# Attention over 8 images: filler products before the first projection, and exact weights for VectorE's low parts kept in an idle bank of sums

## The chip, the core and the metric

One NeuronCore of a Trainium2 chip runs the whole program. The time is the device time of one execution in microseconds; it is compared by medians over several executions of each kernel.

## The reference, cut to what matters

For each of 8 images with 128 channels and 32 x 32 = 1024 pixels, the program computes self-attention over the pixels:

```python
q = einsum('oc,bcn->bon', Wq, xf) + bq      # 64 x 1024 per image
k = einsum('oc,bcn->bon', Wk, xf) + bk      # 64 x 1024
v = einsum('oc,bcn->bon', Wv, xf) + bv      # 128 x 1024
attn = softmax(einsum('bci,bcj->bij', q, k), axis=-1)   # 1024 x 1024
out  = gamma * einsum('bcn,bmn->bcm', v, attn) + x
```

All inputs and the output are fp32.

## The kernel before, in words

TensorE works with rounded fp32r and bf16 operands, so each factor is split into a high part and a low part (the rest). An exponential is therefore made twice by ScalarE: `weight` (exact, fp32) and `weight_hi` (rounded to fp32r). Their difference, `weight_lo` (bf16), is made by GpSimd (POOL) in three steps of four and by VectorE (DVE) in the fourth.

**The work.** There are 128 steps, 16 for each image. A step `s` has 2 tiles of keys by 256 queries, 512 columns of scores in all. Four steps make a part `u` (`PART_STEPS` = 4): a part has 256 queries, and its sums fill two of the four PSUM banks called `sums`: banks 0 and 1 for even `u`, 2 and 3 for odd `u` (`part_banks`). The PSUM has 8 banks: two of `scores`, four of `sums`, two of `work`.

**One step.** TensorE makes the scores (`score_tile`, L592 and L593: four products of 256 columns). ScalarE makes the exact weights (L776) and the rounded ones (L779). POOL (L469) or DVE (L878) subtracts. TensorE adds the high parts to the sums two steps later (`sums_hi`, L612: four products of 258 columns), and once per part all four low parts (`sums_lo`, L626: sixteen products of 130 columns). DVE has the low part of step 2 of each part from part 1 on (`low_on_dve`, 31 steps); POOL has the other 97.

**Beside it.** Softmax needs the largest score of each row first. TensorE makes the high scores of a later chunk into a bank of `work` (L548, 120 products of 512 columns) and DVE takes the maximum (L840). Further jobs on the two banks of `work` are the projections of the next images: q and k (L535 to L537) and v (L542). A bank is handed on when DVE has read it, so TensorE waits for DVE there. The steps 0 to 17 have more maxima than the later ones, up to two each (`EARLY_MAXES`), because the maxima run ahead by nearly two chunks.

**Order.** Each engine has its own list, written out by the step loop `for s in range(ALL_STEPS)`. In loop `s` TensorE does the scores of step `s + 2`, the maxima of `max_jobs(s)`, `sums_hi(s - 2)`, and, where `s - 2` ends a part, `sums_lo`; then side jobs. ScalarE does both exponentials of step `s + 2`. DVE does side jobs, the maxima of loop `s`, then `low_weights(s + 1)` where that step is its own, then `invert` and `add_low` of a part that has just ended (L889, L883), then `finish` (L903), which writes the output tile and counts `y_done`. `sums_hi` of the first step of part `u` waits until part `u - 2`, the last user of its banks, has been finished (`y_done`).

**The start.** POOL sets `identity` (a memset L420, then a select L422); TensorE waits for it and turns it `WARM_UP` = 10 times into bank 0 of `sums` (`keep_busy`, L632), a transpose of 128 columns each. Then come the first three projections k0, q0, k1 (L641: fp32 products of 512 columns, each two instructions, when the loads of x and of the weights have landed), whose results ScalarE takes up (L790, L794). VectorE has nothing to do until k0 has been taken up.

Of the kernel before, what the change touches and what calls it, by code (L numbers as in the profile page):

```python
# [11 lines left out]
HALVES = PIXELS // CHUNK  # L12
# [8 lines left out]
PAIR = 2  # L21
PART = PAIR * TILE
PARTS = CHUNKS * CHUNK_TILES // PAIR
PART_STEPS = ALL_STEPS // PARTS
# [7 lines left out]
IDENTITY_MADE = 2  # L32
SETUP_MADE = 14

WARM_UP = 10

FIRST = ["k0", "q0", "k1", "q1"]

# [1 line left out]
DVE_LOW = 2  # L40
# [55 lines left out]
def low_on_dve(s):  # L96
    return s >= PART_STEPS and s % PART_STEPS == DVE_LOW


def low_count(s):  # L100

    return sum(low_on_dve(i) == low_on_dve(s) for i in range(s + 1))
# [27 lines left out]
def half_count(n, h):  # L130

    return HALVES * (n - 1) + h + 1
# [6 lines left out]
def wait(engine, semaphore, count):  # L139
    if count > 0:  # L140
        engine.wait_ge(semaphore, count)


def attention_program(nc, x, x_turned, w_turned, biases, bv, gamma, out):
    fp32 = mybir.dt.float32
    fp32r = mybir.dt.float32r
    bf16 = mybir.dt.bfloat16
    ALU = mybir.AluOpType
    ACT = mybir.ActivationFunctionType
# [4 lines left out]
    with ExitStack() as ctx:  # L154
        def sbuf(name, shape, dtype):
            return ctx.enter_context(nc.sbuf_tensor(name, shape, dtype))

        def psum(name, shape, dtype):
            return ctx.enter_context(nc.psum_tensor(name, shape, dtype))

        def sem(name):
            return ctx.enter_context(nc.semaphore(name))

        identity = sbuf("identity", [128, 128], fp32)
        identity_r = sbuf("identity_r", [128, 128], fp32r)
        w_v_plain = sbuf("w_v_plain", [CHANNELS, CHANNELS], fp32)
        w_qk_t = sbuf("w_qk_t", [CHANNELS, 2 * HEAD], fp32)
# [29 lines left out]
        weight = sbuf("weight", [TILE, RING, CHUNK], fp32)  # L197
        weight_hi = sbuf("weight_hi", [TILE, RING, CHUNK], fp32r)
        weight_lo = sbuf("weight_lo", [TILE, RING, CHUNK], bf16)
# [6 lines left out]
        scores = psum("scores", [TILE, 2, CHUNK], fp32)  # L206
        sums = psum("sums", [TILE, CHUNK_TILES, CHUNK], fp32)
# [16 lines left out]
        pool_setup = sem("pool_setup")  # L224
# [27 lines left out]
        max_rows_done = sem("max_rows_done")  # L252
        max_row_sent = [sem(f"max_row_sent{p}") for p in range(2)]

        first_lo_done = sem("first_lo_done")
        qk_lo_done = sem("qk_lo_done")
        v_lo_done = sem("v_lo_done")
# [2 lines left out]
        weight_lo_done = sem("weight_lo_done")  # L260
# [4 lines left out]
        y_done = sem("y_done")  # L265
# [13 lines left out]
        def part_tile(kt, it):  # L279

            return slice(kt * PART + it * TILE, kt * PART + (it + 1) * TILE)

        def part_banks(u):
            return slice(u % 2 * PAIR, (u % 2 + 1) * PAIR)

        def key_tile(s, kt):
            return s % PART_STEPS * PAIR + kt
# [30 lines left out]
        def wait_low(engine, s):  # L318
            engine.wait_ge(weight_lo_done if low_on_dve(s) else weight_lo_pool_done, low_count(s))

        def wait_lo_summed(engine, s):

            if s >= 0:
                engine.wait_ge(sums_done, s // PART_STEPS + 1)
# [182 lines left out]
        def _(pe):  # L507
# [88 lines left out]
            def sums_hi(s):  # L596
                b, k = divmod(s, STEPS)
                u, j, p, r = s // PART_STEPS, s % PART_STEPS, b % 2, s % RING
                if k in (0, 2):
                    if b > 0:  # L600
                        pe.wait_ge(v_lo_done, half_count(b, k // 2))
                    elif k == 0:
                        pe.wait_ge(first_v_lo_done, 1)
                    else:
                        pe.wait_ge(first_v_rest_done, 1)
                if j == 0:

                    wait(pe, y_done, PAIR * (u - 1))
                pe.wait_ge(weight_hi_done, s + 1)
                for kt in range(PAIR):  # L610
                    for it in range(PAIR):
                        last = pe.matmul(sums[:, u % 2 * PAIR + it, 0:VCOLS], weight_hi[:, r, part_tile(kt, it)],  # L612
                                         values[p][:, key_tile(s, kt)], start=(j == 0 and kt == 0), stop=False)
                last.then_inc(hi_step, 1)
# [14 lines left out]

            def keep_busy(turns, place):  # L630
                for _ in range(turns):
                    pe.transpose(place[:, 0:128], identity[:, :], identity[:, :])  # L632

            pe.wait_ge(pool_setup, IDENTITY_MADE)
            keep_busy(WARM_UP, sums[:, 0])

            def project_first(name):
# [47 lines left out]
            for s in range(ALL_STEPS + LAG):  # L685
                if s + AHEAD < ALL_STEPS:
                    score_tile(s + AHEAD)
                if s < ALL_STEPS:
                    for c, i in max_jobs(s):
                        do_max(c, i)  # L690
                if s < PART_STEPS:
                    if s == 0:

                        pe.wait_ge(neg_max_done, CHUNK_TILES + PAIR)
                    sums_hi(s)
                elif PART_STEPS + LAG <= s < ALL_STEPS:
                    if s == PART_STEPS + LAG:

                        pe.wait_ge(qk_lo_done, HALVES)
                    sums_hi(s - LAG)  # L700
                if LAG <= s < ALL_STEPS and (s - LAG) % PART_STEPS == PART_STEPS - 1:
                    sums_lo(s - LAG)
                if s == 1:
                    pe.wait_ge(neg_max_done, MAXES)
                    project_qk(1, 0, sums[:, PAIR + 1])
                if s == 2:
                    pe.wait_ge(first_v_rest_done, 1)
                    project_qk(1, 1, sums[:, PAIR])
                if s < ALL_STEPS:
                    for job in side_jobs(s):  # L710
                        do_job(job)


            p, u = (BATCHES - 1) % 2, PARTS - 1
            pe.wait_ge(weight_hi_done, ALL_STEPS)
            for it in range(PAIR):
                place = sums[:, u % 2 * PAIR + it]
# [13 lines left out]
        def _(act):  # L731
# [39 lines left out]
            def exponentials(s):  # L771
                r = s % RING
                act.wait_ge(scores_done, s + 1)
                if s >= RING:
                    wait_low(act, s - RING)
                act.activation(weight[:, r], scores[:, s % 2], ACT.Exp)  # L776

                wait(act, hi_step, s - RING + 1)
                act.activation(weight_hi[:, r], scores[:, s % 2], ACT.Exp).then_inc(weight_hi_done, 1)  # L779

            def take_low_sum(u):
                act.wait_ge(sums_done, u + 1)

                wait(act, total_done, u - 1)
                act.activation(low_sum[:, u % 2], sums[:, part_banks(u), 0:CHANNELS], ACT.Copy).then_inc(low_sum_done, 1)  # L785
# [19 lines left out]
            act.wait_ge(pool_setup, SETUP_MADE)  # L805
            write_max_rows(1, 0, 0, PART, bank(0))
            exponentials(0)
            first_q(1, bank(0))
            round_v(0, 1, sums[:, PAIR])
            exponentials(1)  # L810

            for s in range(ALL_STEPS):
                b, k = divmod(s, STEPS)
                if s + AHEAD < ALL_STEPS:
                    exponentials(s + AHEAD)
                if s in (1, 2):
                    round_qk(1, s - 1, sums[:, PAIR + 2 - s])
                if s >= LAG and (s - LAG) % PART_STEPS == PART_STEPS - 1:
                    take_low_sum((s - LAG) // PART_STEPS)
                for job in side_jobs(s):  # L820
                    do_job(job)
                if k in X_HI_STEPS and b + 2 < BATCHES:
                    round_x(b + 2, X_HI_STEPS.index(k))
# [4 lines left out]
        def _(dve):  # L828
# [45 lines left out]
            def low_weights(s):  # L874
                r = s % RING
                dve.wait_ge(weight_hi_done, s + 1)
                wait_lo_summed(dve, s - RING)
                dve.tensor_tensor(weight_lo[:, r], weight[:, r], weight_hi[:, r], ALU.subtract).then_inc(weight_lo_done, 1)  # L878

            def add_low(u):  # L880
                dve.wait_ge(low_sum_done, u + 1)
                place = sums[:, part_banks(u), CHANNELS:2 * CHANNELS]
                dve.tensor_tensor(place, place, low_sum[:, u % 2], ALU.add).then_inc(total_done, 1)  # L883

            def invert(u):
                dve.wait_ge(low_sum_done, u + 1)

                wait(dve, y_done, PAIR * (u - 1))
                dve.reciprocal(one_over[:, u % 2], sums[:, part_banks(u), 2 * CHANNELS]).then_inc(one_over_done, 1)  # L889

            def finish(u):
# [9 lines left out]
                for it in range(PAIR):  # L901
# [2 lines left out]
                                             one_over[:, u % 2, it:it + 1], x_turned_sb[:, n % TURNED, h * CHUNK_TILES + at],  # L904
                                             ALU.mult, ALU.add).then_inc(y_done, 1)

            dve.wait_ge(biases_loaded, 16)

            def first_lo(h):
# [32 lines left out]
            for s in range(ALL_STEPS):  # L942
# [10 lines left out]
                if s >= LAG and (s - LAG) % PART_STEPS == PART_STEPS - 1:  # L953
                    u = (s - LAG) // PART_STEPS
# [6 lines left out]
            u, half = PARTS - 1, 1  # L961
# [54 lines left out]
```

## Time and profile before

| | |
|---|---|
| median of 3 executions | 231.02 us (230.31 to 231.49) |
| the profiled execution, its own time | 231.92 us |
| its span, first to last instruction | 230.1 us |
| TensorE (PE) busy | 223.4 us, 97% |
| POOL busy | 189.1 us, 82% |
| ScalarE (ACT) busy | 177.9 us, 77% |
| VectorE (DVE) busy | 168.2 us, 73% |

Busy time of PE is from a model of its pipeline, so a busy PE need not be at its peak. PEld is the loading of weights into the array, which runs beside the products. In the chain of waits each piece is what held up the next one, followed back from the end; a stretch that is PE alone is one in which no other engine was late. The column of the granted TensorE clock shows 1.00 in every slice of the page.

### The profile page before, as it was taken

How to read it: one execution, taken by the hardware profiler on the slowest of the kernel's cores; microseconds unless marked ns; L12 is line 12 of the kernel's file. 1: busy time of each engine (PE TensorE's matmuls, PEld its weight loads, DVE VectorE, ACT ScalarE, POOL GpSimd, SP SyncE). 2: the span in 40 equal slices, each digit the busy share in tenths (PEclk: the TensorE clock that was granted, in tenths of full speed). 3: DMA queues.
4: the chain of work that ended last, by engine and by line, in shares of the span. 5: the costliest groups of instructions: out<-in, count | busy, mean ns of one | idle time of the engine just before them, and what ended most of it. 6: DMA issues, size and time to landing. Idle time of an engine off the chain costs nothing.

```text
span 230.1 us, 5324 instructions
## 1 busy us (share of the span) xinstructions
PE 223.4 (97%) x1858; PEld 204.8 (89%) x1858; DVE 168.2 (73%) x339; ACT 177.9 (77%) x342; POOL 189.1 (82%) x163
## 2 busy tenths in 40 slices
PE   7999989999999999999999999999999999999994
PEld 4477868999999999999999999999999999999994
DVE  0586869976878878868897778768887777776544
ACT  2578967777887888877887788878887878878980
POOL 8668888696998979987798979989799878799871
PEclk9999999999999999999999999999999999999999
DMA  5571940096406770195504961076302951100111
GB/s 151 143 265 28 203 137 4 2 229 166 157 3 160 159 231 0 15 232 133 178 0 93 226 171 63 2 184 141 140 0 35 231 153 43 47 0 3 46 50 46
DMA packets 17978, 24.56 MB, mean 107 GB/s; under 512 B 9760, under 2 KB 10784, under 8 KB 17952
## 3 DMA queue, kind: packets, MB, share of 16 engines
q1 hardware_dynamic: 17520, 24.03, 40.9%
q8 instruction: 15, 0.25, 0.4%
q10 hardware_dynamic: 432, 0.20, 0.3%
q14 instruction: 11, 0.09, 0.1%
HBM read 8.72 MB, written 4.19 MB: 56 GB/s over the span
## 4 chain that ended last, share of the span: by engine, by line
PE 88%; DVE 5%; ACT 2%; DMA 2%; issue 1%; SPq 1%; POOL 0%; POOLq 0%; ACTq 0%
PE sums L612 24%; PE scores L592 13%; PE scores L593 12%; PE work L548 12%; PE sums L626 12%; PE work L542 5%; DMA k_hilo<-qk_lo 2%; DVE neg_max L840 2%; PE work L535 1%; PE scores L641 1%; PE work L537 1%; PE work L536 1%; PE work L641 1%; PE sums L632 1%; DVE weight_lo L878 1%
## 5 line engine op out<-in xcount | busy, mean ns | idle before, releaser
L469 POOL TENSOR_TENSOR weight_lo<-weight,weight_hi 128x512 bf16<-128x512 f32 x97 | 134.9, 1406 | 22.3 <-ACT weight_hi L779 21.5
L840 DVE TENSOR_REDUCE neg_max<-work 128x1 f32<-128x512 f32 x120 | 81.4, 683 | 4.7 <-PE work L548 4.7
L776 ACT ACTIVATE weight<-scores 128x512 f32<-128x512 f32 x128 | 76.7, 599 | 9.5 <-PE scores L593 1.8
L612 PEld LDWEIGHTS sums<-values,weight_hi 128*128 128x128 f32 x504 | 76.8, 189 | 5.0
L612 PE MATMUL sums<-values,weight_hi 128*128 128x258 f32 x504 | 80.7, 282 | 0.0
L779 ACT ACTIVATE weight_hi<-scores 128x512 fp32r<-128x512 f32 x128 | 76.8, 600 | 0.0
L592 PE MATMUL scores<-q_hihi,k_hilo 128*128 128x256 f32 x256 | 71.0, 300 | 0.2 <-ACT q_lomax L760 0.2
L593 PE MATMUL scores<-q_lomax,k_hione 128*128 128x256 f32 x256 | 66.2, 281 | 0.0
L548 PE MATMUL work<-k_hilo,q_hihi 128*128 128x512 f32 x120 | 49.0, 413 | 0.8 <-DVE neg_max L840 0.5
L592 PEld LDWEIGHTS scores<-q_hihi,k_hilo 128*128 128x128 f32 x256 | 48.2, 188 | 1.6 <-issue 0.9
L593 PEld LDWEIGHTS scores<-q_lomax,k_hione 128*128 128x128 f32 x256 | 48.5, 189 | 1.1 <-issue 0.5
L878 DVE TENSOR_TENSOR weight_lo<-weight,weight_hi 128x512 bf16<-128x512 f32 x31 | 32.4, 1044 | 6.1 <-ACT weight_hi L779 6.1
L626 PE MATMUL sums<-values_b,weight_lo 128*128 128x130 bf16 x496 | 34.4, 221 | 0.0
L626 PEld LDWEIGHTS sums<-values_b,weight_lo 128*128 128x128 bf16 x496 | 28.9, 98 | 1.5 <-issue 0.2
L548 PEld LDWEIGHTS work<-k_hilo,q_hihi 128*128 128x128 f32 x120 | 22.4, 188 | 3.3 <-DVE neg_max L840 1.1
L450 POOL TENSOR_TENSOR x_lo<-x_sb,x_hi 128x512 fp32r<-128x512 f32 x12 | 15.3, 1276 | 10.4 <-ACT x_hi L751 10.4
L785 ACT ACTIVATE low_sum<-sums 128x256 f32<-128x256 f32 x31 | 11.9, 384 | 15.0 <-PE sums L626 15.0
L836 DVE TENSOR_TENSOR values<-work,values 128x512 fp32r<-128x512 f32 x14 | 9.7, 692 | 17.3 <-ACT values L755 17.3
L477 POOL TENSOR_TENSOR x_turned_sb<-x_turned_sb,gamma_bv 128x512 f32<-128x512 f32 x16 | 20.6, 1289 | 0.0
L903 DVE SCALAR_TENSOR_TENSOR y_sb<-sums,one_over,x_turned_sb 128x128 f32<-128x128 f32 x62 | 18.5, 339 | 0.7 <-DVE sums L883 0.4
L831 DVE SCALAR_TENSOR_TENSOR qk_lo<-work,all_biases,qk_hi 128x512 fp32r<-128x512 f32 x12 | 9.0, 751 | 11.6 <-ACT qk_hi L744 11.6
L755 ACT ACTIVATE values<-work 128x512 fp32r<-128x512 f32 x14 | 8.4, 600 | 9.0 <-PE work L542 9.0
(72 smaller groups left out, 158.4 us busy)
## 6 DMA issues: line engine op xcount, KB each, us to landing
x_turned_sb<-in_x_turned SPq DMA_DIRECT2D x8, 512.0 KB, 5.0
out<-y_sb SPq DMA_DIRECT2D x15, 256.0 KB, 2.7
x_sb<-in_x SPq DMA_DIRECT2D x7, 512.0 KB, 4.4
q_hihi<-qk_hi SPq DMA_DIRECT2D x12, 256.0 KB, 4.4
q_lomax<-qk_lo SPq DMA_DIRECT2D x7, 256.0 KB, 5.7
k_hione<-qk_hi SPq DMA_DIRECT2D x7, 256.0 KB, 5.6
k_hilo<-qk_hi SPq DMA_DIRECT2D x6, 256.0 KB, 3.2
k_hilo<-qk_lo SPq DMA_DIRECT2D x6, 256.0 KB, 5.7
```

The source lines that it names most:

```text
L469: pool.tensor_tensor(weight_lo[:, r], weight[:, r], weight_hi[:, r], ALU.subtract).then_inc(weight_lo_pool_done, 1)
L477: pool.tensor_tensor(place, place, bias, ALU.add).then_inc(with_bias_done, 1)
L548: pe.matmul(place, q_hihi[p][:, tile(t)], k_hilo[p][:, chunk(h)], start=True, stop=True).then_inc(mx_done, 1)
L592: pe.matmul(place, k_hilo[p][:, keys], q_hihi[p][:, queries], start=True, stop=False)
L593: last = pe.matmul(place, k_hione[p][:, keys], q_lomax[p][:, queries], start=False, stop=True)
L612: last = pe.matmul(sums[:, u % 2 * PAIR + it, 0:VCOLS], weight_hi[:, r, part_tile(kt, it)], values[p][:, key_tile(s, kt)], start=(j == 0 a ...
L626: last = pe.matmul(sums[:, u % 2 * PAIR + it, CHANNELS:VCOLS], weight_lo[:, i % RING, part_tile(kt, it)], values_b[p][:, key_tile(i, kt)], ...
L776: act.activation(weight[:, r], scores[:, s % 2], ACT.Exp)
L779: act.activation(weight_hi[:, r], scores[:, s % 2], ACT.Exp).then_inc(weight_hi_done, 1)
L840: dve.reduce_max(neg_max[:, t, h:h + 1], place, AX.X, negate=True).then_inc(neg_max_done, 1)
L878: dve.tensor_tensor(weight_lo[:, r], weight[:, r], weight_hi[:, r], ALU.subtract).then_inc(weight_lo_done, 1)
L903: dve.scalar_tensor_tensor(y_sb[:, h, at], sums[:, u % 2 * PAIR + it, CHANNELS:2 * CHANNELS], one_over[:, u % 2, it:it + 1], x_turned_sb[: ...
```

## The change

Five things change.

1. `filler`, a tile of 128 x 128 fp32, is set to 1.0 by DVE as its first instruction. TensorE waits for that and no longer for the identity.
2. `keep_busy` issues ordinary products of `filler` by `filler` in place of transposes of the identity, and 15 of them in place of 10.
3. For the steps whose low part is DVE's, ScalarE writes the exact weights to PSUM, into the second bank of the two that hold the sums of the step's own part (`exact_weights`), and DVE reads them there. The rounded weights stay in SBUF.
4. For these steps ScalarE waits, before the exact exponential, until part `u - 2` is finished (`y_done`), and in part 1 also until both halves of the second image's q and k have been taken out of `sums` (`qk_lo_done`).
5. TensorE waits, before the first `sums_hi` of each part from part 1 on, until DVE has made the low part of that part's step 2 (`weight_lo_done`), since that product overwrites the bank.

```diff
-WARM_UP = 10
+WARM_UP = 15
...
+        filler = sbuf("filler", [128, 128], fp32)
...
+        filler_set = sem("filler_set")
...
+        def exact_weights(s):
+
+            return sums[:, s // PART_STEPS % 2 * PAIR + 1]
...
                 if j == 0:
 
                     wait(pe, y_done, PAIR * (u - 1))
+                    if u > 0:
+                        pe.wait_ge(weight_lo_done, low_count(s + DVE_LOW))
                 pe.wait_ge(weight_hi_done, s + 1)
...
             def keep_busy(turns, place):
                 for _ in range(turns):
-                    pe.transpose(place[:, 0:128], identity[:, :], identity[:, :])
-
-            pe.wait_ge(pool_setup, IDENTITY_MADE)
+                    pe.matmul(place[:, 0:128], filler[:, :], filler[:, :], start=True, stop=True)
+
+            pe.wait_ge(filler_set, 1)
             keep_busy(WARM_UP, sums[:, 0])
...
                 if s >= RING:
                     wait_low(act, s - RING)
-                act.activation(weight[:, r], scores[:, s % 2], ACT.Exp)
+                if low_on_dve(s):
+                    u = s // PART_STEPS
+                    wait(act, y_done, PAIR * (u - 1))
+                    if u == 1:
+                        act.wait_ge(qk_lo_done, HALVES)
+                act.activation(exact_weights(s) if low_on_dve(s) else weight[:, r], scores[:, s % 2], ACT.Exp)
...
-                dve.tensor_tensor(weight_lo[:, r], weight[:, r], weight_hi[:, r], ALU.subtract).then_inc(weight_lo_done, 1)
+                dve.tensor_tensor(weight_lo[:, r], exact_weights(s), weight_hi[:, r], ALU.subtract).then_inc(weight_lo_done, 1)
...
+            dve.memset(filler[:, :], 1.0).then_inc(filler_set, 1)
             dve.wait_ge(biases_loaded, 16)
```

## Rows read from the trace of the kernel before

**Rows 1.** Page, part 4: chain that ended last, shares by engine.

```profile
PE 88%; DVE 5%; ACT 2%; DMA 2%; issue 1%; SPq 1%; POOL 0%; POOLq 0%; ACTq 0%
```

**Rows 2.** Windows of 10 us: length, busy PE, PEld, DVE, ACT, POOL, clock, DMA.

```profile
60.00:70.00 10.00, 10.00 (x79) 9.15 (x78) 7.74 (x16) 8.71 (x17) 9.50 (x9) 1.00 0.06 10
...
210.00:220.00 10.00, 10.00 (x101) 9.91 (x100) 4.88 (x12) 9.07 (x19) 8.13 (x7) 1.00 0.10 26
```

**Rows 3.** Chain of waits at the start: start us, us, what.

```profile
1.52 2.39 PE sums L632 x10
3.91 2.05 PE scores L641 x2
5.96 1.71 PE work L641 x2
7.66 1.04 PE scores L641 x2
...
14.38 0.86 PE work L641 x2
```

**Rows 4.** Timeline, POOL, 0 to 2 us: start us, us, engine, line, operation.

```profile
0.72 0.20 POOL L420 MEMSET identity<- 128x128 f32 x1 [0.29 <-POOLq L997]
```

**Rows 5.** By line, L878, L836 and L469: count, shortest/median/longest ns.

```profile
L878 DVE TENSOR_TENSOR weight_lo<-weight,weight_hi x31: 681/1173/1616, 27.2 to 222.8; 128x512 bf16<-128x512 f32 x31
...
L836 DVE TENSOR_TENSOR values<-work,values x14: 691/692/694, 32.5 to 206.8; 128x512 fp32r<-128x512 f32 x14
...
L469 POOL TENSOR_TENSOR weight_lo<-weight,weight_hi x97: 1273/1294/1753, 15.1 to 223.9; 128x512 bf16<-128x512 f32 x97
```

**Rows 6.** Page, part 5: busy us, mean ns, idle before, releaser.

```profile
L878 DVE TENSOR_TENSOR weight_lo<-weight,weight_hi 128x512 bf16<-128x512 f32 x31 | 32.4, 1044 | 6.1 <-ACT weight_hi L779 6.1
```

**Rows 7.** Timeline, 32 to 33 us: DVE's subtraction beside one of POOL.

```profile
32.11 1.31 POOL L477 TENSOR_TENSOR x_turned_sb<-x_turned_sb,gamma_bv 128x512 f32<-128x512 f32 x1
...
32.55 0.69 DVE L836 TENSOR_TENSOR values<-work,values 128x512 fp32r<-128x512 f32 x1 [1.29 <-ACT values L755]
```

**Rows 8.** Chain of waits, 27 to 38 us.

```profile
27.25 1.30 DVE weight_lo L878
...
30.72 1.17 PE work L542 x8
...
35.72 0.82 DVE weight_lo L878
...
37.65 0.50 PE work L535
```

**Rows 9.** Timeline, 26.9 to 29 us: part 1's low part and PE beside it.

```profile
27.16 1.39 DVE L878 TENSOR_TENSOR weight_lo<-weight,weight_hi 128x512 bf16<-128x512 f32 x1
...
27.53 0.66 PEld L612 LDWEIGHTS sums<-values,weight_hi 128*128 128x128 f32 x4
...
28.72 0.40 PE L548 MATMUL work<-k_hilo,q_hihi 128*128 128x512 f32 x1
```

**Rows 10.** Timeline, parts 6 and 28: low part, and the first load of `sums_hi`.

```profile
64.35 1.21 DVE L878 TENSOR_TENSOR weight_lo<-weight,weight_hi 128x512 bf16<-128x512 f32 x1
...
65.30 0.66 PEld L612 LDWEIGHTS sums<-values,weight_hi 128*128 128x128 f32 x4
...
208.92 0.69 DVE L878 TENSOR_TENSOR weight_lo<-weight,weight_hi 128x512 bf16<-128x512 f32 x1
...
209.75 0.54 PEld L612 LDWEIGHTS sums<-values,weight_hi 128*128 128x128 f32 x4
```

**Rows 11.** Chain of waits: two projections of v in the long PE stretch.

```profile
100.55 0.89 PE work L542 x8
...
107.19 1.15 PE work L542 x8
```

**Rows 12.** Timeline, 23 to 25 us: second half of q and k, and step 6's exponential.

```profile
23.23 0.75 DVE L831 SCALAR_TENSOR_TENSOR qk_lo<-sums,all_biases,qk_hi 128x512 fp32r<-128x512 f32 x1 [0.50 <-ACT qk_hi L744]
...
24.17 0.60 ACT L776 ACTIVATE weight<-scores 128x512 f32<-128x512 f32 x1
```

## The prediction, made before the changed kernel had run

> **What bounds the kernel now.** I read the chain of waits first. By engine it is PE for 88%, DVE for 5% and POOL for nothing [rows 1]. The windows then tell where the rest lies: from 60 us on PE is busy without a gap, as the first and the last of these 16 windows show [rows 2]. So work that is taken from DVE or POOL there saves nothing by itself. What can be saved lies in two places: the start, where the chain goes through fillers and projections [rows 3], and the stretch up to 38 us, where the early maxima make DVE late and two of its low parts stand on the chain [rows 8]. One more stall stands inside the long PE stretch: eight instructions of the v projection take 0.89 us there, but once 1.15 [rows 11].
>
> The clock must be read from durations. The column of the granted clock says 1.00 throughout, but an fp32 product of 512 columns takes 1.71 us at 5.96 and 0.86 at 14.38 [rows 3]: two to one, the levels of 1.2 and 2.4 GHz. The third projection takes 1.04, between the two, so the clock rose inside it: 0.37 us at the low level and 0.67 at the high one make one product, which puts the rise at 7.66 + 0.37 = 8.0 us, 4.1 us after the first product began at 3.91 and 6.5 us after the first transpose at 1.52.
>
> **Part 1, the fillers.** Removed are ten transposes (2.39 us) behind POOL's memset and select. A memset of the same size is done at 0.92 on POOL [rows 4]; DVE has nothing ahead of it, so I take the first filler at 1.0 us in place of 1.52 (estimate). An fp32 product of 128 columns is a quarter of one of 512: 1.71 / 4 = 0.43 us at the low level, and 0.89 / 4 = 0.22 at the high one, since eight instructions of L542 are four such products [rows 3, 11]. Fifteen are 6.4 us or 3.3 us. So all hangs on when the clock rises. I take the delay that the trace shows after true products, 4.1 us: the rise is at 5.1, 9.5 fillers are done by then, the other 5.5 take 1.2, and they end at 6.3. The loads are no bound, since the first projection began at 3.91. Three projections at 0.86 are 2.6, and 0.2 passes until a result is out (the first piece, 2.05, has 0.34 over 1.71, of which I take somewhat over half): k1 is out at 9.1 instead of 8.70. **+0.4 us**, all on the chain: ScalarE, the first maxima and the first scores hang on k1. From below: were the delay only half (2.0 us), 4.7 fillers would be done at 3.0 and 10.3 more take 2.3, which ends at 5.3: k1 at 8.1, -0.6. From above: all fillers at the low level end at 7.45, k1 at 10.2, +1.5.
>
> **Part 2, DVE's subtraction.** With both operands in SBUF it took 681 to 1616 ns, median 1173 [rows 5], 32.4 us in all with a mean of 1044 [rows 6]. A subtraction of the same size with one operand in PSUM took 691 to 694 in all 14 cases, also where POOL ran its own beside it for the whole time [rows 5, 7]. I take 0.69 for all 31. From below 0.68, the shortest of L878; from above 1.6, the longest. DVE is spared 31 x 0.35 = 11 us of work. POOL's rows (median 1294, longest 1753) should settle at about 1.29 [rows 5]. After 60 us both gains lie beside PE and are worth nothing, but for the stall at 107: the low part just before it was one of the longest, and without it the projection has 0.89: **-0.25 us** (0 to -0.3).
>
> The Trainium skill's "VectorE: DVE Perf Modes", in the section on the TRN2 errata, gives a DVE instruction 58 fixed cycles from SBUF and 120 from PSUM, which speaks against the move: it would be about 0.06 us longer, an estimate from that page. The rows show 0.01 between the shortest L878 and L836 [rows 5], so I keep the rows; by the page the total would be some 0.1 us worse.
>
> **Part 3, the stretch from 27 to 38 us.** The low part of part 1 ends at 27.16 + 0.69 = 27.85 instead of 28.55 [rows 9]. Now TensorE waits for it: its first load for that part's sums stood at 27.53 [rows 9], so it is 0.35 us late, and everything behind it in PE's order with it, the next maximum product from 28.72 to 29.08. That product lasts 0.4, so DVE's maximum can start at 29.5 and its 0.68 ends at 30.2. The v projection that waits for this bank starts then instead of 30.72: -0.5 rather than the full 0.7, since the new wait takes back 0.2. The second low part on the chain has 0.82 there; at 0.69, less the 0.08 by which DVE's instructions overlap here, it would have 0.61. Of the 0.2 I keep half, since PE's own work comes next, so the projection at 37.65 starts at 37.05 [rows 8]. **-0.6 us** in all, at most -0.9 (both in full, no wait), at least -0.2.
>
> **Part 4, the added waits elsewhere.** Behind PE's new wait stand all its later scores and maxima, and ScalarE behind those. In part 6 the low part would end at 64.35 + 0.69 = 65.04 and PE loads at 65.30: 0.26 to spare [rows 10]. In part 28 it is 209.75 - 209.61 = 0.14, the tightest after the first [rows 10]. The others repeat 0.26 (ten times) or 0.47 (twelve times) with few exceptions; part 12's low part, the one before the stall at 107, started late beside POOL, which goes with the contention. A handoff between engines costs a few hundredths, so I cost these waits at nothing; the cover is PE's scores and one maximum, and it is gone once the subtraction is longer than 0.9 us. Behind ScalarE's new wait stand the rounded exponentials. In part 1 it needs the second half of q and k, out at 23.98, and its exponential started at 24.17 [rows 12]: free by 0.19. In later parts it needs a finish that lies two parts back, over a microsecond earlier. An exponential into PSUM is not in the trace: I take 0.60 as into SBUF [rows 12], between 0.5 and 0.7 (estimates); ScalarE is not on the chain after 60 us.
>
> **Sum.** +0.4 - 0.6 - 0.25 = -0.45, rounded to -0.5: 231.92 becomes 231.4 for the profiled execution. That execution was 0.9 over the median of 231.02, so the forecast for the median is **230.5 us**. What a measurement of this kernel can tell from no change is about 0.5%, or 1.2 us; the forecast lies inside.
>
> **The rivals.**
>
> *The clock rises early.* The rise follows the fillers by only half the delay, so start and early stretch both gain: -0.6 - 0.6 - 0.25 = -1.5, 229.5 us. For it: one execution shows one delay. Against: two whole projections did run at the low level. Chance 0.24, faster.
>
> *The clock counts from PE's first activity, transposes too.* Then 6.5 us are due again, and the rise at 7.5 comes after all fillers: +1.5 - 0.85 = +0.65, 231.7 us. For it: the rise at 8.0 fits either count. The Trainium skill's "TensorE: Matmul & The Clock Gate", in Part 4, says that transposes do not count as activity for the clock as products do; by that page this rival falls. No row here decides it. Chance 0.14, mostly the same.
>
> *DVE's subtraction stays slow, and the new wait turns that into a stall.* It decides where the subtraction passes 0.95 us (0.69 + 0.26). At 1.2 us, part 6's own value [rows 10], PE loses 0.25 in each of the ten parts with 0.26 to spare, 0.04 in the twelve with 0.47, and some 0.4 in each of parts 1, 2, 12 and 28: 4.6 us, over the start's +0.4 about 236 us. For it: `weight_hi` still comes from SBUF. Against: 14 rows at 691 to 694 beside POOL [rows 5, 7]. Chance 0.07, slower. A smaller kin, the late clock with no early gain, gives 232.5: chance 0.03.
>
> **How the numbers follow.** The forecast has 0.52, all of it within 0.5%. Faster 0.24 (early clock), same 0.52 + 0.14 = 0.66, slower 0.07 + 0.03 = 0.10. The range reaches from the early clock with the full early gain, -0.6 - 0.9 - 0.3 = -1.8 (229.2), to the late clock with a small one, +1.5 - 0.4 = +1.1 (232.1); the subtraction that stays slow is left out.
>
> **What would show it.** Right: L878 at 0.69 in all 31 rows, POOL's L469 near 1.29, PE without a gap from 60 us on, the v projection at 107 at 0.89, k1 taken up between 8.6 and 9.5 us, and the first projections at 0.86. Part 1's sums should load right after its low part. Wrong: projections or fillers at the low level to their end; PE idle before L612 once per part; ScalarE waiting for `y_done`; L878 spread as before.

## The result and the profile after

The changed kernel takes **231.86 us** (median of 20 executions, 231.18 to 232.50) against 231.15 (20 executions, 230.31 to 231.98). The ratio is 1.0033, with an interval of 1.0018 to 1.0049: slower by a third of a per cent, where 230.5 had been forecast. Inside half a per cent, as the chances had it, but on the other side of the old median and clear of noise.

The first thing to see is that the two profiled executions say the opposite: 231.81 after, 231.92 before, and spans of 230.0 and 230.1. Read alone, they would make the change worth a tenth of a microsecond. The explanation lies in that contradiction, so it comes before any reading of engines.

The chain of waits of the changed kernel at the start (start us, us, what) answers to [rows 3]:

```profile
0.82 0.18 DVE filler L920
...
1.05 5.74 PE sums L640 x30
6.79 0.86 PE scores L649 x2
7.65 0.86 PE work L649 x2
8.51 0.87 PE scores L649 x2
...
9.40 0.69 ACT k_hilo L803
```

The 15 fillers (30 instructions) begin at 1.05 and hold TensorE until 6.79. All three projections then run at the high level, 0.86 each where before they took 2.05, 1.71 and 1.04 [rows 3], and still ScalarE takes up k1 only at 9.40. In the profiled execution of before that was at 8.72.

DVE's subtraction and POOL's, by line (count, shortest/median/longest ns), and on the page (busy us, mean ns, idle before), against [rows 5, 6]:

```profile
L891 DVE TENSOR_TENSOR weight_lo<-sums,weight_hi x31: 680/691/693, 27.8 to 222.7; 128x512 bf16<-128x512 f32 x31
```

```profile
L475 POOL TENSOR_TENSOR weight_lo<-weight,weight_hi 128x512 bf16<-128x512 f32 x97 | 123.7, 1289 | 30.7 <-ACT weight_hi L792 30.2
```

Here everything is as forecast: DVE takes 0.68 to 0.69 us in all 31 rows, and POOL's mean is 1.29, the median of before, whose tail to 1.75 is gone (the longest is 1.31). The page's busy time falls from 168.2 to 158.7 us for DVE and from 189.1 to 177.9 for POOL. None of it is seen in the time, since from 60 us on PE is busy without a gap, as it was (windows, against [rows 2]):

```profile
60.00:70.00 10.00, 10.00 (x79) 9.19 (x78) 7.20 (x16) 8.70 (x18) 8.71 (x8) 1.00 0.07 16
210.00:220.00 10.00, 10.00 (x101) 9.91 (x100) 3.86 (x11) 9.15 (x19) 7.58 (x7) 1.00 0.10 26
```

ScalarE's exponential takes as long into PSUM as into SBUF (changed kernel, by line):

```profile
L789 ACT ACTIVATE weight<-scores x97: 579/598/628, 14.6 to 222.6; 128x512 f32<-128x512 f32 x97
L789 ACT ACTIVATE sums<-scores x31: 582/595/634, 24.9 to 221.6; 128x512 f32<-128x512 f32 x31
```

The new wait bites once, in part 1, as forecast (timeline of the changed kernel, against [rows 9]):

```profile
27.85 0.68 DVE L891 TENSOR_TENSOR weight_lo<-sums,weight_hi 128x512 bf16<-128x512 f32 x1
28.21 0.39 PE L554 MATMUL work<-k_hilo,q_hihi 128*128 128x512 f32 x1
...
28.60 0.54 PEld L620 LDWEIGHTS sums<-values,weight_hi 128*128 128x128 f32 x4 [0.32 <-issue]
```

The first load for part 1's sums starts 0.07 us after the low part has ended, after 0.32 us of idle. In the other parts PE loads 0.23 us or more after the low part.

And the stall at 107 us is gone (chain, against [rows 11]):

```profile
100.65 0.89 PE work L548 x8
...
107.30 0.89 PE work L548 x8
```

So by these two traces the start loses 0.68 us (k1 at 9.40 for 8.72), the stretch up to 52 us gives back 0.55 (its rows stand at part 3 below) and the stall 0.27. How, then, are the medians 0.7 apart?

### The profile page after: what moved, and what is told of

The parts are those of the page before. It is cut to its first block, busy times and chain, and to the rows that moved or that the text cites. A ratio compares the mean times of both kernels' runs of the same rounds, so it can differ in the third digit from the quotient of the medians.

```text
span 230.0 us, 5373 instructions
## 1 busy us (share of the span) xinstructions
PE 224.3 (98%) x1878; PEld 207.5 (90%) x1878; DVE 158.7 (69%) x340; ACT 178.4 (78%) x342; POOL 177.9 (77%) x163
## 3 DMA queue, kind: packets, MB, share of 16 engines
HBM read 8.72 MB, written 4.19 MB: 56 GB/s over the span
## 4 chain that ended last, share of the span: by engine, by line
PE 89%; DVE 4%; ACT 3%; DMA 2%; SPq 1%; issue 1%; ACTq 0%
PE sums L620 25%; PE scores L598 13%; PE sums L634 12%; PE work L554 12%; PE scores L599 12%; PE work L548 5%; PE sums L640 2%; DMA k_hilo<-qk_lo 2%; PE work L541 1%; DVE neg_max L853 1%; PE work L543 1%; PE work L542 1%; PE scores L649 1%; PE work L649 1%; PE sums L537 1%
## 5 line engine op out<-in xcount | busy, mean ns | idle before, releaser
L475 POOL TENSOR_TENSOR weight_lo<-weight,weight_hi 128x512 bf16<-128x512 f32 x97 | 123.7, 1289 | 30.7 <-ACT weight_hi L792 30.2
L789 ACT ACTIVATE weight<-scores 128x512 f32<-128x512 f32 x97 | 58.0, 598 | 9.4 <-PE scores L599 2.2
L891 DVE TENSOR_TENSOR weight_lo<-sums,weight_hi 128x512 bf16<-128x512 f32 x31 | 21.3, 687 | 5.9 <-ACT weight_hi L792 5.9
L789 ACT ACTIVATE sums<-scores 128x512 f32<-128x512 f32 x31 | 18.4, 595 | 0.2
```

Of the source, the lines that this page charges most:

```text
L475: pool.tensor_tensor(weight_lo[:, r], weight[:, r], weight_hi[:, r], ALU.subtract).then_inc(weight_lo_pool_done, 1)
L789: act.activation(exact_weights(s) if low_on_dve(s) else weight[:, r], scores[:, s % 2], ACT.Exp)
L891: dve.tensor_tensor(weight_lo[:, r], exact_weights(s), weight_hi[:, r], ALU.subtract).then_inc(weight_lo_done, 1)
```

## The experiments

Two theories. **A**: the fillers cost the time, and the profiled execution of before hides it, because its start was one of the worst of that kernel. **B**: the weights in PSUM cost the time, through the new waits or the exponentials into PSUM, and the traces of single executions hide that.

### The two halves of the change, each alone, and fewer fillers

Fillers alone: the changed kernel with the PSUM weights and the waits that came with them undone (points 3 to 5 of the change).

```diff
-                act.activation(exact_weights(s) if low_on_dve(s) else weight[:, r], scores[:, s % 2], ACT.Exp)
+                act.activation(weight[:, r], scores[:, s % 2], ACT.Exp)
...
-                dve.tensor_tensor(weight_lo[:, r], exact_weights(s), weight_hi[:, r], ALU.subtract).then_inc(weight_lo_done, 1)
+                dve.tensor_tensor(weight_lo[:, r], weight[:, r], weight_hi[:, r], ALU.subtract).then_inc(weight_lo_done, 1)
```

> The kernel before with the 15 filler products alone; the exact weights stay in SBUF. Theory A: the fillers cost the time. The profiled execution of before had a late clock rise (8.0 us) and was slow, 231.92 against a median of 231.15, so its usual start is some 0.8 us better than the rows showed, while 15 fillers hold the projections until 5.8 to 7.5 us whatever the clock does. After lost 0.7 in the median although its later stages gained 0.55 and 0.25, so the fillers alone cost 1.5 us: 232.6, ratio about 1.0065. Theory B: the PSUM weights cost the time (their new waits, or the exponentials into PSUM), and the fillers are neutral: ratio 1.000 to 1.002.

Measured: 232.28 us, ratio 1.0058 (1.0038 to 1.0079).

PSUM weights alone: the changed kernel with the ten transposes of the identity put back, and no memset on DVE.

```diff
-WARM_UP = 15
+WARM_UP = 10
...
-                    pe.matmul(place[:, 0:128], filler[:, :], filler[:, :], start=True, stop=True)
+                    pe.transpose(place[:, 0:128], identity[:, :], identity[:, :])
...
-            pe.wait_ge(filler_set, 1)
+            pe.wait_ge(pool_setup, IDENTITY_MADE)
...
-            dve.memset(filler[:, :], 1.0).then_inc(filler_set, 1)
```

> The kernel before with the exact weights of DVE's steps in PSUM alone; ten transposes of the identity as before. Theory A: the early stretch gains 0.55 and the stall at 107 us 0.25, so -0.8 us: 230.35, ratio about 0.9965. Theory B: ratio 1.002 or more. In both, DVE's subtraction is 0.69 us and POOL's 1.29.

Measured: 230.33 us, ratio 0.9980 (0.9962 to 0.9999).

The changed kernel with 7 and with 10 fillers (`WARM_UP = 7`, `WARM_UP = 10`).

> The changed kernel with 7 filler products in place of 15. At the low level they take 3.0 us, from 1.05 to about 4.0, when the loads of x and of the first weights have landed (the first projection of before began at 3.9). Theory A: the projections no longer wait for fillers, the clock rises at about the same times as in the changed kernel, and the start is some 0.3 us better than that of before: with the 0.8 of the PSUM part ratio about 0.995 to before (230.0 us), some 1.9 us better than with 15. Theory B: no better than 1.002. A third theory, C, in which all 15 are needed to raise the clock: the rise comes late, after 8 us, and the time is no better than with 15.

Measured: 230.68 us, ratio 0.9976 (0.9957 to 0.9996).

> The changed kernel with 10 filler products, which last until 4.7 to 5.3 us. Theory A: between the two, each filler that is taken away after the loads have landed gives 0.22 to 0.43 us: about 1.1 to 1.2 us better than with 15, ratio 0.998 to 0.999 to before. Theory C: a late rise here too, 1.003 or worse. Theory B: 1.002 or more.

Measured: 230.58 us, ratio 0.9981 (0.9963 to 1.0000).

Theory B is out: the PSUM weights alone are faster, the fillers alone slower, and neither interval reaches 1. Theory C is out too, since 10 and 7 fillers are as good as or better than before. For theory A the sizes were partly off. From 15 fillers to 10 the gain was 1.2 us by the ratios, as expected. With 7, a ratio of 0.995 had been expected and 0.9976 came, no better than with 10. The chain shows that the seven fillers last 3.35 us, not 3.0, and hold the first projection until 4.40; whether that is the whole difference is not shown.

```profile
1.05 3.35 PE sums L640 x14
4.40 1.71 PE scores L649 x2
```

The PSUM weights gave 0.5 us by the ratio where 0.8 was expected; 0.25 of the 0.8 belongs elsewhere, as the next runs show.

### No fillers, four, and two refinements

No filler and 4 fillers: `WARM_UP = 0` and `WARM_UP = 4` in the changed kernel.

> The changed kernel with no filler at all; TensorE idles until the loads have landed at 3.9 us. In the changed kernel and its variants the time is 222.4 us more than the moment at which ScalarE takes up k1 (231.81 - 9.40, 230.57 - 8.16, 230.22 - 7.76). Theory D: work on TensorE ahead of the projections is what brings the clock's rise forward, so without it the rise comes after 7 us, two or three projections run at the low level, k1 is taken up at 8.3 to 9.3, and the time is about 231.5, ratio 1.001 to 1.003. Theory E: the fillers do nothing for the clock, its rise falls somewhere between 4.5 and 7.9 us whatever TensorE did, and the time is that of the best start so far: 230.2, ratio 0.996.

Measured: 231.64 us, ratio 1.0015 (1.0001 to 1.0030).

> The changed kernel with 4 filler products, which end at 2.8 us, with 1.1 us of idle before the projections. Theory D: a rise somewhat later on average than with 7, k1 taken up at 7.5 to 9, time 230.9 or more, ratio 0.999 to 1.001. Theory E: 230.2, ratio 0.996.

Measured: 231.60 us, ratio 1.0018 (1.0002 to 1.0035).

Theory E is out. Without fillers the time is about 0.9 us worse, by the ratios, than with 7 or 10 of them, and 15 are no better than none. Four had been expected to be a little better than none (0.999 to 1.001) and are not; why is open. In the chain of the kernel without fillers the third projection still begins at the low level:

```profile
3.81 2.04 PE scores L649 x2
5.85 1.71 PE work L649 x2
7.56 1.21 PE scores L649 x2
...
8.79 0.69 ACT k_hilo L803
```

The other two runs refine the faster half. First, ten transposes as before, with PSUM weights and with a DVE memset that nobody waits for (with its tile and its semaphore):

```diff
-            dve.wait_ge(biases_loaded, 16)
+            dve.memset(filler[:, :], 1.0).then_inc(filler_set, 1)
+            dve.wait_ge(biases_loaded, 16)
```

> The PSUM weights with ten transposes of the identity as before, and DVE's memset as its first instruction, which nobody waits for. In the two kernels without that memset (the kernel before, and the PSUM weights alone) DVE starts the low part of part 12 by 0.29 us late with nothing to wait for, and TensorE loses 0.23 to 0.27 us; in the three with it there is no such delay. If one more instruction at DVE's head moves that delay away, part 12's low part follows L866 by 0.08 us, and the time is 0.25 us better than the PSUM weights alone: 230.1, ratio 0.9955 to 0.997. If not, the delay stands where it was and the time is 230.33.

Measured: 230.67 us, ratio 0.9978 (0.9961 to 0.9996). The time does not show the 0.25 us, but the trace shows what was asked. DVE's timeline around part 12's low part: in the kernel before, with the PSUM weights alone, and with the memset, in this order:

```profile
104.12 0.16 DVE L855 TENSOR_REDUCE neg_max_r<-neg_max 128x4 fp32r<-128x8 f32 x1
104.57 1.57 DVE L878 TENSOR_TENSOR weight_lo<-weight,weight_hi 128x512 bf16<-128x512 f32 x1 [0.29 <-ACT weight_hi L779]
```

```profile
102.36 0.16 DVE L866 TENSOR_REDUCE neg_max_r<-neg_max 128x4 fp32r<-128x8 f32 x1
102.81 0.69 DVE L889 TENSOR_TENSOR weight_lo<-sums,weight_hi 128x512 bf16<-128x512 f32 x1 [0.29 <-ACT weight_hi L790]
```

```profile
103.25 0.16 DVE L868 TENSOR_REDUCE neg_max_r<-neg_max 128x4 fp32r<-128x8 f32 x1
103.34 0.69 DVE L891 TENSOR_TENSOR weight_lo<-sums,weight_hi 128x512 bf16<-128x512 f32 x1
```

The delay of 0.29 us before the low part does not depend on where the weights lie. It is there without the memset and gone with it. (The releaser named had been done for over a microsecond.) It is gone with the fillers alone too, where the weights lie in SBUF, and there the same subtraction takes 0.69 us in place of 1.57:

```profile
105.03 0.16 DVE L857 TENSOR_REDUCE neg_max_r<-neg_max 128x4 fp32r<-128x8 f32 x1
105.12 0.69 DVE L880 TENSOR_TENSOR weight_lo<-weight,weight_hi 128x512 bf16<-128x512 f32 x1
```

The kernel with the memset instead lost 0.2 us in part 28, in idle time that the timeline puts down to issue, and that was not followed further.

Second, on top of that, the new wait put off until TensorE needs the bank that holds the weights:

```diff
                     wait(pe, y_done, PAIR * (u - 1))
-                    if u > 0:
-                        pe.wait_ge(weight_lo_done, low_count(s + DVE_LOW))
...
-                for kt in range(PAIR):
-                    for it in range(PAIR):
...
+                for n in range(PAIR * PAIR):
+                    kt, it = (n % PAIR, n // PAIR) if j == 0 else (n // PAIR, n % PAIR)
+                    if j == 0 and n == PAIR and u > 0:
+                        pe.wait_ge(weight_lo_done, low_count(s + DVE_LOW))
...
```

> As the kernel with PSUM weights and memset, with the new wait put off: in the first step of a part TensorE makes both products of the bank that holds no weights, waits for the low part, and then makes those of the other bank. If the wait in part 1 costs 0.25 us (TensorE stood still there from 28.4 to 28.6 in the changed kernel), that goes: some 229.9, 0.1 to 0.25 better than without. If DVE's next maximum is what holds the chain, nothing changes there. All other parts unchanged, as they had 0.23 us or more to spare.

Measured: **230.12 us, ratio 0.9958 (0.9942 to 0.9974)**, the lowest median of the study, and lower than that of the kernel before and of the changed one. Its timeline shows that the load in part 1 no longer waits for the low part to end:

```profile
25.59 0.68 DVE L891 TENSOR_TENSOR weight_lo<-sums,weight_hi 128x512 bf16<-128x512 f32 x1
25.95 0.39 PE L554 MATMUL work<-k_hilo,q_hihi 128*128 128x512 f32 x1
25.96 0.67 PEld L620 LDWEIGHTS sums<-values,weight_hi 128*128 128x128 f32 x4
```

From k1 to the end of the early stretch this is worth 0.16 us in its trace (42.49 us against 42.65 in the changed kernel and in the one without the split). The rest of the difference to the run without the split is not shown to come from it: the two intervals overlap, and their starts scatter as described next.

### The same kernels again

> The kernel before, unchanged, one more profiled execution. Theory A: the first profile had one of the latest clock rises (8.0 us by its durations), and others of the same kernel rise anywhere from some 4.7 to 8 us; ScalarE takes up k1 between 7.1 and 8.8 us, and the time is 223.2 us more than that moment (231.92 - 8.72), or 222.95 where the delay in part 12 is missing. Against it: the rise stands at 8.0 again, and the time differs for another cause.

Measured: 231.42 us.

> As for the execution before it: k1 between 7.1 and 8.8 us, the time 223.2 (or 222.95) more than that; not the same rise in all three.

Measured: 231.79 us.

> The changed kernel, unchanged, one more profiled execution. Theory A: the time is 222.4 us more than the moment of k1 (231.81 - 9.40), and k1 is taken up between 8.8 and 10.1 us, since the fillers end at 6.0 at the earliest; never as early as the kernel before can be.

Measured: 231.72 us.

> As for the execution before it: k1 between 8.8 and 10.1 us, the time 222.4 more.

Measured: 231.52 us.

All four came as theory A had it: k1 lies in the ranges given, and the time is 223.2 or 222.4 us more. Two chains of waits show the scatter: the kernel before, again (its rise is 1 us earlier than in [rows 3]), and the fastest kernel, whose start has the same ten transposes and the earliest rise of any kernel with them.

```profile
1.51 2.39 PE sums L632 x10
3.91 1.92 PE scores L641 x2
5.83 1.47 PE work L641 x2
7.30 0.87 PE scores L641 x2
8.19 0.69 ACT k_hilo L790
```

```profile
1.51 2.39 PE sums L640 x10
3.91 1.48 PE scores L649 x2
5.39 0.86 PE work L649 x2
6.25 0.87 PE scores L649 x2
7.14 0.69 ACT k_hilo L803
```

A projection at the low level is 1.71, the first with its entry 2.05 (1.92 to 2.07 in the other chains). Each microsecond at the high level does the work of two, so what a projection falls short of that is how long it ran at the high level. In the first chain the second projection is short by 1.71 - 1.47 = 0.24, so the clock rose at 7.30 - 0.24 = 7.1 us; in the second the first one is short by 0.57, so it rose at 4.8. Over all profiled executions, in the same way:

| kernel | time of that execution | clock rises | k1 taken up | time less k1 |
|---|---|---|---|---|
| before | 231.92 | 8.0 | 8.72 | 223.20 |
| before, again | 231.42 | 7.1 | 8.19 | 223.23 |
| before, again | 231.79 | 7.8 | 8.56 | 223.23 |
| fillers alone | 232.65 | in the fillers | 9.62 | 223.03 |
| after | 231.81 | in the fillers | 9.40 | 222.41 |
| after, again | 231.72 | in the fillers | 9.30 | 222.42 |
| after, again | 231.52 | in the fillers | 9.10 | 222.42 |
| PSUM weights alone | 230.18 | 5.6 | 7.53 | 222.65 |
| with memset | 231.03 | 7.4 | 8.39 | 222.64 |
| with memset, split wait | 229.56 | 4.8 | 7.14 | 222.42 |
| 10 fillers | 230.22 | in the fillers | 7.76 | 222.46 |
| 7 fillers | 230.57 | 6.7 | 8.16 | 222.41 |
| 4 fillers | 231.72 | 9.0 | 9.26 | 222.46 |
| none | 231.29 | 8.3 | 8.79 | 222.50 |

The traces also keep a record of the clock, which begins with the rise. In it the high level begins 0.0 to 0.2 us ahead of the moments in the table (at 7.9, 6.9 and 7.6 us in the three executions of before, at 4.8 in the fastest kernel), and it places the rises that fall inside the fillers: 6.0 us with the fillers alone, 5.5, 5.3 and 4.9 in the three executions of after, 4.4 with ten fillers.

The last column is the finding. Behind k1 the two kernels that were run again take the same time to within 0.03 us in each of their three executions, and nearly all that is left of the scatter is the moment of k1, which the clock sets. And the last column falls by 0.8 us from before to after: the part of the change that was meant to pay did.

The medians can now be read back. Before: 231.15 - 223.2 = 7.95, the moment of k1 in a usual execution, between 7.1 (230.31) and 8.8 (231.98). After: 231.86 - 222.4 = 9.45, between 8.8 and 10.1. The start loses **1.5 us**, the rest gains **0.8**, and 0.7 is what was measured. Theory A holds.

The 1.5 is worked out from medians; no pair of traces shows it. All three profiled executions of before lie above its median and all three of after below theirs, so their k1 are only 0.8 us apart in the mean (8.49 and 9.27). The fillers alone bear the larger figure out: 232.28 - 223.03 puts their k1 at 9.25, 1.3 us over 7.95.

## Why the prediction was wrong, point by point

**The step that failed is the last one of the sum**: "That execution was 0.9 over the median of 231.02, so the forecast for the median is 230.5". The difference of -0.5 had been worked out against the k1 of one execution, 8.70 in the chain, and was then taken off the median as if the 0.9 lay in something that the change leaves alone. It lay in the very term that the change replaces: behind k1 the kernel before takes 223.20 to 223.23 us in all three executions, so the 0.77 us by which that execution stands over the median of twenty (231.15) are its late start. Of the 1.36 us by which 230.5 missed 231.86, some 1.1 are this one term (+1.5 in the place of +0.4), and 0.13 are the median of three executions, 231.02, in the place of that of twenty. Against its own execution the forecast was 231.4, and the profiled execution after had 231.8; three of them mean 231.68.

**Part 1, the fillers.** "+0.4 us" was mis-sized for the median: 1.5 us. The chain of the changed kernel itself was forecast well (fillers to 6.3 and k1 out at 9.1; found 6.48, 6.68 and 6.79, and 9.10, 9.30 and 9.40). The delay of 4.1 us was near the mark there too: by the clock's record the rise came 3.9 to 4.5 us after the first filler. What was wrong is the other side of the subtraction, and with it the reading of the delay "4.1 us after the first product" as a property of the kernel before. With the same ten transposes the rise came 0.9 to 4.1 us after the first product. The first filler at 1.0 was right (1.05), and so were 0.43 and 0.22 per filler.

**Part 2, DVE's subtraction.** Right: 0.69, and POOL at 1.29. Wrong in one place: the stall at 107 was put down to the long subtraction before it. Its cause is the delay of 0.29 us ahead of it, which stands in the kernel with the PSUM weights alone too and goes with the memset, so the -0.25 belongs to the fillers' side of the change. Where the delay stays, the short subtraction does not save the time: TensorE then idles for 0.25 us at the new wait.

```profile
103.72 0.54 PEld L618 LDWEIGHTS sums<-values,weight_hi 128*128 128x128 f32 x4 [0.25 <-issue]
```

The size of -0.25 was right, for the changed kernel, by luck.

**Part 3, the early stretch.** Right: "-0.6" against 0.55, by the stall behind the new wait in part 1 as it was described. The chain of before has the maximum product that waits for the load at 51.92, that of the changed kernel at 52.05; less k1 these are 43.20 and 42.65.

```profile
51.92 0.50 PE work L548
```

```profile
52.05 0.50 PE work L554
```

**Part 4, the waits elsewhere.** Right: the parts named with 0.26 and 0.47 to spare have them still, part 28 has 0.23 for the 0.14 forecast, and ScalarE sat idle for 0.2 us in all ahead of its 31 exponentials into PSUM.

**The rivals.** The early clock was taken for a property of the changed kernel, with a chance of 0.24; the moment of the rise differs from execution to execution in both kernels. That an earlier rise than the profiled one would help the kernel before at least as much was not thought of, and it is the reason why the outcome lay on the other side. The late clock gave 231.7 us, near the measured 231.86, for the wrong reason: no profiled execution after had its rise behind the fillers. The subtraction that stays slow did not come.

**The rule on PSUM operands** from the section on the TRN2 errata in "VectorE: DVE Perf Modes" of the Trainium skill (some 0.06 us more) does not show: the shortest row is 680 ns from PSUM and 681 from SBUF.

## What to carry to other kernels

A profile is one draw. Where the stage that a change replaces can come out in several ways, the median less the profiled time says how that draw stands; work the difference against the median's start, or look at several executions first, and never carry a difference over to the median by subtraction alone. Work that fills a wait should not last long beyond it, and how long is best found by trying: without fillers the first projection begins at 3.81, seven fillers hold it until 4.40 and ten until 5.15, with the same ratio for both (0.9976 and 0.9981), while the five from 10 to 15 cost some 0.24 us each in the median. Why ten are no worse than seven is not shown.

## What had not been expected of the hardware

The moment at which TensorE's clock goes from 1.2 to 2.4 GHz differs by over 3 us between executions that begin alike: by the durations it was 4.8, 5.6, 7.1, 7.4, 7.8 and 8.0 us in six executions, of four kernels, that all began with the same ten transposes from 1.5 us on. The three of the kernel before span 0.9 us of that; its 20 times span 1.67 us, and as half of a delay of the rise shows in the time, that would be some 3.3 us in the rise (an estimate). The column of the granted clock does not show it; it has a 9 in all 40 slices of the page, and in the windows it reads 1.00 from the first on (changed kernel, 0 to 2 us, while the fillers run at the low level):

```profile
0.00:2.00 2.00, 0.95 (x4) 0.95 (x5) 0.17 (x1) 0.34 (x1) 1.09 (x9) 1.00 0.11 20
```

Transposes bring the rise forward. Without work ahead of the projections it came 4.5 us after the first product, in the one execution profiled, at 8.3; with ten transposes it was earlier in all six above, once only 0.9 us after the first product. The medians say the same: 231.64 us without work, 230.67 with the transposes and the memset, or k1 at 9.1 and 8.0 by the last column of the table. Against seven fillers, which end later (4.40 against 3.91), ten transposes are no worse, with ratios of 0.9976 and 0.9978. "TensorE: Matmul & The Clock Gate" of the Trainium skill says in Part 4 that transposes do not count as activity for the clock as products do; in these runs they do as much as the fillers, and the runs decide.

One more instruction at the head of DVE's list (a memset, with its tile and its semaphore) took away a delay of 0.29 us a hundred microseconds later. Why is open; the delay stood in all three executions of the kernel before and in that of the PSUM weights alone, and in none of the ten with the memset.
